# Image convolution block on one core: F(4,3) for two of three convolutions, and the next band's attention begun a step early

## The reference

```python
stk = _neighborhood(x)                        # the 9 shifted views
q = einsum('bhwd,de->bhwe', x, Q_P)
k = einsum('bhwkd,de->bhwke', stk, K_P)
v = einsum('bhwkd,de->bhwke', stk, V_P)
scores = einsum('bhwke,bhwe->bhwk', k, q) * mask
alpha = softmax(scores, axis=-1)
t = x + einsum('bhwk,bhwke->bhwe', alpha, v)
t_in = t
t = relu(conv(t, ff1_kernel) + ff1_bias)      # 64 -> 64
t = relu(conv(t, ff2_kernel) + ff2_bias)      # 64 -> 128
t = relu(conv(t, ff3_kernel) + ff3_bias)      # 128 -> 64
return t_in + t
```

## Time and profile before

| | |
|---|---|
| time, median of 3 runs | 2644.49 us (2639.14 to 2647.08) |
| time of the profiled execution | 2641.18 us |
| its span, first to last instruction | 2639.0 us |
| TensorE matmul busy | 2451.5 us, 93% of the span |
| VectorE busy | 1892.5 us, 72% |
| ScalarE busy | 1183.0 us, 45% |
| mean granted TensorE clock | 0.978 of 2.4 GHz |
| DMA | 311.68 MB, mean 118 GB/s |

### The profile page before, as it was taken

The page is one execution under the profiler, slowest core; times in us unless marked ns, Lnnn a source line. Parts: engine busy times, 40 slices in busy tenths (PEclk is TensorE's granted clock), DMA queues, the critical chain, the costliest instruction groups (busy, mean ns, idle before and its releaser), DMA issues.

```text
span 2639.0 us, 54500 instructions
## 1 busy us (share of the span) xinstructions
PE 2451.5 (93%) x19992; PEld 1300.4 (49%) x19992; DVE 1892.5 (72%) x2767; ACT 1183.0 (45%) x3171; POOL 15.4 (1%) x23
## 2 busy tenths in 40 slices
PE   5999999998899999999889999999988999999997
PEld 3545554554455555545354555455445554554543
DVE  4777777775577777777667777777756777777775
ACT  2544444543454444444344444444435444544433
POOL 2000000000000000000000000000000000000000
PEclk7999999999899999999989999999999999999999
DMA  4433443443344434433244344344423443444343
GB/s 117 134 117 114 121 132 107 124 129 99 98 128 126 132 100 118 140 115 116 87 135 120 109 121 134 112 119 126 133 78 118 122 133 107 123 129 124 107 121 99
DMA packets 217442, 311.68 MB, mean 118 GB/s; under 512 B 15460, under 2 KB 149412, under 8 KB 210724
## 3 DMA queue, kind: packets, MB, share of 16 engines
q1 hardware_dynamic: 217324, 310.12, 40.6%
HBM read 135.47 MB, written 33.82 MB: 64 GB/s over the span
## 4 chain that ended last, share of the span: by engine, by line
PE 71%; DVE 15%; issue 8%; ACT 4%; DVEq 1%; DMA 0%; SPq 0%; ACTq 0%
PE conv_banks L430 26%; PE conv_banks L444 18%; PE conv_banks L407 9%; DVE work L736 6%; PE conv_banks L411 4%; DVE dtl L714 3%; PE mix_bank L384 3%; PE score_banks L369 3%; PE mix_bank L395 3%; ACT dth L606 3%; PE score_banks L358 2%; DVE tf L685 2%; DVE work L698 2%; PE score_banks L350 1%; PE score_banks L366 1%
## 5 line engine op out<-in xcount | busy, mean ns | idle before, releaser
L444 PE MATMUL conv_banks<-du,w2f 64*128 64x512 f32 (+2 forms) x3264 | 745.9, 588 | 57.6 <-DVE work L736 49.0
L430 PE MATMUL conv_banks<-dodd,w3f 128*64 128x512 f32 (+1 forms) x1656 | 499.0, 577 | 10.8 <-DVE dodd L698 10.8
L430 PE MATMUL conv_banks<-deven,w3f 128*64 128x512 f32 (+1 forms) x1656 | 492.0, 567 | 4.2 <-DVE deven L698 3.7
L444 PEld LDWEIGHTS conv_banks<-du,w2f 64*128 64x128 f32 x3264 | 294.7, 190 | 377.6 <-issue 256.4
L533 ACT ACTIVATE prob<-score_banks,negmax 128x100 f32<-128x100 f32 x1040 | 344.9, 360 | 177.8 <-DVE negmax L665 177.8
L726 DVE TENSOR_TENSOR work<-conv_banks,m_sb 128x512 f32<-128x512 f32 (+3 forms) x273 | 179.7, 658 | 327.3 <-PE conv_banks L444 262.6
L736 DVE TENSOR_TENSOR work<-conv_banks,work 128x1024 f32<-128x1024 f32 (+3 forms) x273 | 312.3, 1165 | 60.2 <-PE conv_banks L430 40.6
L563 ACT COPY m_sb<-conv_banks 128x512 f32<-128x512 f32 (+3 forms) x273 | 146.9, 564 | 376.4 <-PE conv_banks L430 165.1
L606 ACT CAST dth<-work 128x1024 fp32r<-128x1024 f32 x130 | 136.1, 1047 | 303.0 <-DVE work L698 302.0
L430 PEld LDWEIGHTS conv_banks<-deven,w3f 128*64 128x64 f32 x1656 | 171.8, 137 | 155.0 <-issue 109.3
L430 PEld LDWEIGHTS conv_banks<-dodd,w3f 128*64 128x64 f32 x1656 | 149.0, 136 | 189.5 <-issue 148.8
(11 more groups left out here) (82 smaller groups left out, 2719.3 us busy)
## 6 DMA issues: line engine op xcount, KB each, us to landing
xk<-x_keys SPq DMA_DIRECT2D x66, 800.0 KB
xc<-x_bands SPq DMA_DIRECT2D x67, 650.0 KB, 5.5
dodd<-dodd SPq DMA_DIRECT2D x68, 512.0 KB, 2.9
xr<-x_bands SPq DMA_DIRECT2D x264, 128.0 KB, 4.8
kept<-tf SPq DMA_DIRECT2D x129, 256.0 KB, 5.0
out<-work SPq DMA_DIRECT2D x60, 512.0 KB, 2.6
dth<-dth SPq DMA_DIRECT2D x68, 256.0 KB, 2.3
dtl<-dtl SPq DMA_DIRECT2D x68, 256.0 KB, 2.4
```

What stands on the lines that cost most here:

```text
L430: return nc.tensor.matmul(bank[rows, lo * 128:hi * 128], w3f[:, m, s, odd * C:odd * C + C], source[:, lo + s // 2:hi + s // 2, m], start=s ...
L444: return nc.tensor.matmul(conv_banks[:, bank_of(which, j), lo * 128:hi * 128], w2f[rows, STREAMS[j], 2 * (which == EVEN) + s], du[rows, lo ...
```

## The change

Convolutions 1 and 2 go from F(2,3) to F(4,3): six streams of a quarter of the width, two to a bank, so three banks instead of four, and four outputs of six products. Both multiply whole fp32; the high and low parts of convolution 1 are gone. VectorE forms the six streams from a first set of differences (`differences`) and then `outer4`, `far4` and `near4`, and the four outputs with `u_middle`, `u_four`, `u_outer` (convolution 1) and `y_middle`, `y_four`, `y_outer` (convolution 2, even and odd rows in one operation). Convolution 3 stays as it was, in its own buffer (`sums3`). r and the first scores of the next band are made in the step before (`nxt`), the r product now in the scores' banks. ScalarE multiplies the probabilities by the inverted sums (`norm`, one copy with a scale for each of four patches), VectorE only inverts (`invert`). The sum with x is one operation. The shared counters `dve_read` and `relu_done` become one semaphore for each use.

The order of each engine, and the new functions, cut to the core:

```diff
             def step(G, k, b, q, par, att):      # SP
-                sp.wait_ge(tile_done, filled(G, CONV1, 3))
-                for t in (dth, dtl):
-                    sp.dma_start(t[:, 0:1].bitcast(F32), t[:, RP:RP + 1].bitcast(F32)).then_inc(t_kept, 16)
+                sp.wait_ge(tile_done, filled(G, CONV1, 2))
+                sp.dma_start(dt[:, :, 0:1], dt[:, :, RP:RP + 1]).then_inc(t_kept, 16)
...
-                store(G, k)
                 if att:
                     sp.wait_ge(mixed, b * 2 + 2)
                     load_xk(b + 1)
-                    sp.wait_ge(t_ready, b * 2 + 2)
+                store(G, k)
+                if att:
+                    sp.wait_ge(t_ready, b + 1)
...
-                sp.wait_ge(tile_done, filled(G, EVEN, 3))
-                sp.dma_start(du[:, 0:1], du[:, RP:RP + 1]).then_inc(u_kept, 16)
+                sp.wait_ge(tile_done, filled(G, EVEN, 2))
+                sp.dma_start(du[:, :, 0:1], du[:, :, RP:RP + 1]).then_inc(u_kept, 16)
```

```diff
+            def conv1_pair(G, k, b, j):          # TensorE
+                if j == 0:
+                    pe.wait_ge(y_mid, before(G))
+                    pe.wait_ge(dt_done, b * 5)
+                    pe.wait_ge(t_kept, G * 16 + 16)
+                elif j == 2:
+                    pe.wait_ge(y_out, before(G))
+                bank = conv_banks[:, BANK1[j]]
+                taps = [(1, 1, 0, RP), (0, 0, 1 if k == 0 else 0, RP)] if k < BANDS else [(0, 0, 0, 1)]
+                for m in range(2):
+                    for n, s, lo, hi in taps:
+                        last = nc.tensor.matmul(bank[:, m * 256 + lo * 64:m * 256 + hi * 64], w1f[:, 2 * j + m, n],
+                                                dt[:, 2 * j + m, lo + s:hi + s],
+                                                start=m == 0 and n == taps[0][0], stop=m == 1 and n == 0)
+                last.then_inc(tile_done, 1)
...
             def begin2(G, k, j):
                 if j == 0:
                     pe.wait_ge(act_read, act_reads(G, CONV3))
+                    pe.wait_ge(o_mid, this(G))
+                    pe.wait_ge(du_done, G * 5 + 10)
+                elif j == 1:
+                    pe.wait_ge(o_out, this(G))
+                else:
                     pe.wait_ge(act_read, act_reads(G, EVEN))
+                for m in range(2):
+                    for s in range(2):
+                        even = tap2(k, EVEN, j, m, LOWER, s, m == 0 and s == 0, False)
+                        odd = tap2(k, ODD, j, m, UPPER, s, m == 0 and s == 0, False)
...
             def end2(G, k, j):
+                pe.wait_ge(half_done, G * 6 + (2 * j + 2))
+                for m in range(2):
+                    odd = tap2(k, ODD, j, m, LOWER, 1, False, m == 1)
+                    even = tap2(k, EVEN, j, m, UPPER, 0, False, m == 1)
```

```diff
+            def norm(b, g):                      # ScalarE
+                act.wait_ge(inv_done, b * GROUPS + (g + 1))
+                for a in range(GROUP):
+                    last = nc.scalar.activation(prob[:, g % 2, a], prob[:, g % 2, a], ACT.Copy,
+                                                scale=expinv[:, g % 2, a:a + 1])
+                last.then_inc(prob_ready, 1)
...
+            def differences(src, slots, done):   # VectorE
+                p = parts_sb[:, :, 0:slots]
+                nc.vector.tensor_tensor(p[:, 1:3], columns(src, slots, 3, 4), columns(src, slots, 1, 2),
+                                        ALU.subtract).then_inc(done, 1)
+                nc.vector.tensor_tensor(p[:, 0:4:3], columns(src, slots, 2, 5), columns(src, slots, 0, 3),
+                                        ALU.subtract).then_inc(done, 1)
+                for n in range(2):
+                    nc.vector.scalar_tensor_tensor(p[:, 4 + n], columns(src, slots, 1 + n), -4.0,
+                                                   columns(src, slots, 3 + n), ALU.mult, ALU.add).then_inc(done, 1)
+            def outer4(to, slots, done):         # one of 2 x 256 elements
+                nc.vector.scalar_tensor_tensor(to[:, 4:6, 1:1 + slots], p[:, 0:2], -4.0, p[:, 2:4],
+                                               ALU.mult, ALU.add).then_inc(done, 1)
+            def far4(to, slots, done):           # two of 256
+                for m, factor in ((3, 2.0), (1, -2.0)):
+                    nc.vector.scalar_tensor_tensor(to[:, m, 1:1 + slots], p[:, 1], factor, p[:, 2],
+                                                   ALU.mult, ALU.add).then_inc(done, 1)
+            def near4(to, slots, done):          # two of 256
+                for m, op in ((2, ALU.add), (0, ALU.subtract)):
+                    nc.vector.tensor_tensor(to[:, m, 1:1 + slots], p[:, 5], p[:, 4], op).then_inc(done, 1)
...
+            def y_middle(G, k):
+                dve.wait_ge(act_read, act_reads(G, EVEN))
+                dve.wait_ge(tile_done, filled(G, EVEN, 1))
+                banks = conv_banks[:, BANK2[1]:BANK2[1] + 2].rearrange("c o (h n) -> c o h n", h=2)
+                nc.vector.tensor_tensor(y_even[:, :, :, at], banks[:, :, :, at], y_copy[:, :, :, at], ALU.add)
+                nc.vector.tensor_tensor(y_odd[:, :, :, at], banks[:, :, :, at], y_copy[:, :, :, at],
+                                        ALU.subtract).then_inc(y_mid, 1)
+            def four(to, even, odd, n, done):    # y_four on 512 elements, u_four on 256
+                if n == 0:
+                    op = nc.vector.tensor_tensor(to(0), even(0), even(1), ALU.add)
+                elif n == 2:
+                    op = nc.vector.scalar_tensor_tensor(to(2), even(1), 4.0, even(0), ALU.mult, ALU.add)
+                else:
+                    op = nc.vector.scalar_tensor_tensor(to(n), odd(1), 2.0 if n == 1 else 8.0, odd(0),
+                                                        ALU.mult, ALU.add)
+                op.then_inc(done, 1)
```

More of the change, by code:

```diff
@@ L403, in conv1_tile @@
                 taps = [(1, 1, 0, RP), (0, 0, 1 if k == 0 else 0, RP)] if k < BANDS else [(0, 0, 0, 1)]
-                pe.wait_ge(dt_high, b * 2 - (1 - part))
-                for w in (w1h, w1l):
+                for m in range(2):
                     for n, s, lo, hi in taps:
-                        nc.tensor.matmul(bank[:, lo * 128:hi * 128], w[:, m, n], dth[:, lo + s:hi + s, m],
-                                         start=w is w1h and n == taps[0][0], stop=False)
-                pe.wait_ge(dt_low, b * 2 - (1 - part))
@@ L565, in relu_conv1, with relu4 @@
+            def relu4(to, rows, src, lo, hi, shift):
+                return nc.scalar.activation(
+                    to[rows, lo:hi, :, 1:1 + W].rearrange("c s i (w n) -> c n s i w", n=4),
+                    src[rows, :, lo * 64:hi * 64].rearrange("c n (s i w) -> c n s i w", i=2, w=WT4),
+                    ACT.Relu, bias=shift)
             def relu_conv1(G, k):
-                act.wait_ge(dve_read, outer_read(G, CONV1))
-                act.wait_ge(d_done[CONV1], parts(G, 1, 1))
+                act.wait_ge(u_summed, G * 4 + 4)
+                act.wait_ge(u_out, this(G))
+                act.wait_ge(du_done, G * 5 + 5)
@@ L729, in outer, with columns @@
-            def outer(G, k, which, behind=0):
-                lo, hi = pairs(which, k)
-                m03 = conv_banks[:, bank_of(which, 2):bank_of(which, 3) + 1:2 if which in (ODD, EVEN) else 1,
-                                 lo * 128:hi * 128]
-                both = sums[which][:, lo:hi].rearrange("c s i (w n) -> c n (s i w)", n=2)
-                dve.wait_ge(tile_done, filled(G, which, 3) if not behind else G * FILLS + (fill_of(which, 3) + 1 - FILLS))
-                dve.wait_ge(dve_read, middle_read(G, which, behind))
-                nc.vector.tensor_tensor(both, m03, both, ALU.add).then_inc(dve_read, 1)
+            def columns(src, slots, *at):
+                if len(at) == 1:
+                    return src[:, 0:slots, :, at[0]:at[0] + W - 3:4]
+                first = at[0] - (at[1] - at[0] == 1)
+                view = src[:, 0:slots, :, first:first + W].rearrange("c s i (w m) -> c m s i w", m=4)
+                return view[:, 1:3] if first < at[0] else view[:, 0:4:3]
@@ L738, in inputs, with o_outer @@
+            def o_outer(G, k):
+                lo, hi = pairs3(k)
+                m03 = conv_banks[:, 2:4, lo * 128:hi * 128]
+                both = sums3[:, lo:hi].rearrange("c s i (w n) -> c n (s i w)", n=2)
+                dve.wait_ge(tile_done, filled(G, CONV3, 3))
+                dve.wait_ge(o_mid, this(G))
+                nc.vector.tensor_tensor(both, m03, both, ALU.add).then_inc(o_out, 1)
             def inputs(G, k, which, part, behind=0):
                 if part == 0:
-                    dve.wait_ge(relu_done, relus(G, which, behind))
```

600 lines of the change are left out of this document (320 added, 280 removed).

## The result

The kernel after takes 2798.01 us (2793.82 to 2801.05) against 2643.05 before: ratio 1.0585, interval 1.0563 to 1.0607. It is 5.9% slower, 155 us, where 2565 us and a gain were forecast; the time is above the range's end of 2690.

The account below looks back on a forecast made before the run. TensorE, busy 93%, bounds the kernel; the new loop sets full steps at 37.9 us. Four pairs give -83, prologue and tail +9: -74 on 2641.2 us makes 2567, stated as 2565, range 2495 to 2690.

Parts of the forecast that it names:

- the cost of the added operations on VectorE and ScalarE: Per step, VectorE net about +1.4 us, to 30 of 38; ScalarE loses high-part casts, gains 16 small scaled copies.
- Rival (d): Longer loop from dearer matmuls, scalar_tensor_tensor, late norm(3) or du: steps 38.5 to 39.8 us, centre 2630; chance 0.22.
- rival (c): TensorE's clock falls behind each step's 2.3 us gap, costing 1 to 4 us a step: 2705 us; chance 0.17.
- The row that warned of it: Old trace: a 1.5 us gap behind 1.3 us of narrow matmuls was followed by a granted clock of 0.50.
- steps 14 and 15: Band steps near an image pair's end, 15 without attention: together 65.7 us instead of 73.9.
- step 16: Band step with one row pair at an image pair's end: about 35.5 us instead of 43.1.
- the loop through scores, maxima, exponentials, copies, y_middle and norm: From next band's scores to turn(0), 6.8 us with TensorE waits of 2.3 and 0.6; full step 37.9 us.
- Convolution 1 in whole fp32: 12 whole fp32 matmuls on 256 columns, 24 instructions at 0.2275 us each: no gain, no loss.
- Convolution 2's pairs: 36 pairs of 256 columns at 0.215 us: 7.75 us a step against 10.3, 2.55 less.
- Rival (b): TensorE stays full if exponentials and copies come early enough: step 35.2 us, 2437 us in all; chance 0.10.
- rival (e): Weight loads not covered by 256-column matmuls: 2.2 us in 64 steps, 2700 us; chance 0.06.
- The sentence of the Trainium skill on loads: Loads overlap running matmuls only when the row group differs; convolution 1 would pay an estimated 2.2 us more a step.

Follow-up runs that it names:

- relu_rows: Kernel after with the relus of convolutions 1 and 2 writing four neighbours, each read from another plane 1 KB apart: 2807.5 us, ratio 1.0619.
- all_dense: Kernel after with relus of convolutions 1 and 2 writing, and VectorE's differences reading, 32 neighbouring elements (columns permuted): 2609.4 us, ratio 0.9876.
- dense_filled: all_dense plus three matmuls of no use in the gap before convolution 2's third pair: 2581.3 us, ratio 0.9766.
- the planes: Kernel after, reordered against the loop, with relu outputs of convolutions 1 and 2 kept as four quarter-width planes: 2490.3 us, ratio 0.9417.
- copies_first: Kernel after with ScalarE's two copies of convolution 2's middle stream moved ahead of the next band's exponentials: 2850.7 us, ratio 1.0781.

## Why the prediction was wrong

The step that failed is the cost of the added operations on VectorE and ScalarE. The prediction counted elements and took the durations of the earlier trace rows for them, the relus as before and the differences as plain sums ("lower bound and choice are the sum's time"). It looked at their number and never at their access patterns. The runs showed 2.16 us for 1.15 (three relus a step, 3.0 us of ScalarE), 1.11 for 0.69 and 0.63 for 0.42 (four and four a step, 2.5 us of VectorE). Taking the sum's time for scalar_tensor_tensor was right where the elements are neighbours (0.417 for 256, 0.683 for 512). Its upper bound, half again as long, about met the strided one, by luck, since the reason for the excess was another; for the relus no bound was set, since they were not taken as changed. Taking the strides away gave 189 of the 233 us by which the time exceeded 2565, and brings it into the stated range (2609); filling the gap alone does not (2754). Rival (d), a longer loop, had the right direction: norm(3) is late, and turn(1) waits 1.45 us for it. It allowed tenths and steps up to 39.8 us; the step became 41.1.

The Trainium skill states the rule (SBUF — State Buffer, Door 1: The DMA port swizzle, the note on SBUF cachelines): lines of 16 bytes, and two touches of a line are needed for full bandwidth. The trace agrees: every fourth fp32 element is one touch a line, and costs 2.16 against 1.15 us. The same note says that one can stride over 4 fp32 elements for free; here exactly that step nearly doubles a relu's time, while a step of 2 (`middle` of the kernel before, 0.689 us for 512) is free, and the measurement decides. relu_rows shows the same cost, 2.12 us, for reads 1 KB apart.

The second error was a chance, not a step: rival (c). Its mechanism, a gap of 2.3 us and then half clock, happened; the sum left it out, at a chance of 0.17. The row that warned of it was nearer than the prediction took it: it read 1.5 us off its window, but the idle time behind the narrow matmuls of the kernel before was 1.77 us, as long as the 1.71 among full-width ones that did no harm:

```profile
1323.03 0.37 PE L366 MATMUL score_banks<-eye_sb 64*128 64x2 f32 x1 [1.77 <-DVE prob L674]
```

The gap filled gives 44 us on the kernel after and 28 on all_dense (2609 to 2581). The price was some 0.7 us a step (44 us over 60 steps) and not 1 to 4, since the matmuls lose some 1.95 us behind a gap (4.74 for 2.79) but half of it only takes the place of the wait for norm(1); in all_dense the fall also comes in only part of the steps. What decides in which steps the clock falls stays open. By the rule of the Trainium skill that the prediction set beside (c) (TensorE: Matmul & The Clock Gate, Why this matters for your kernels) these gaps would be harmless; the falls behind gaps of 2.1 and 2.5 us contradict it.

What is left, 2581 to 2565, is 16 us, or 4 a pair, of errors that partly cancel. In dense_filled a full step is 38.0 us for 37.9 forecast, steps 14 and 15 together 67.1 for 65.7, step 16 38.0 for 35.5, step 0 31.6 for 33 and step 1 35.4 for 35.2; step 16 is the largest miss. So the loop through scores, maxima, exponentials, copies, y_middle and norm was read rightly, and so was that it takes away the gain of TensorE's lighter work: all_dense waits 2.12 us before the third pair (forecast 2.3) and 0.56 before turn(0) (forecast 0.6). In the kernel after the first wait is 2.52, since the strided differences stand before the maximum, which starts 0.6 us behind the scores for 0.2; the second is hidden by the fall of the clock. Reordered against this loop, the same instructions run in 2604, with the planes in 2490. Convolution 1 in whole fp32 costs nothing, 8 matmuls in 1.83 us (1229.12 to 1230.95), 0.229 each for 0.2275. Convolution 2's pairs take 0.232 for 0.215, 0.6 us a step more. `norm` takes 1.2 us for 1.05.

That the full step came out within 0.1 us is partly luck. In dense_filled turn(1) starts 14.62 us after turn(0) (1171.64 to 1186.26), when norm(3) is ready, for the 14.5 forecast; but by then TensorE had been idle for 0.75 us, where the prediction had it arrive at 14.6. Its work ahead of turn(1) was put too high, and the wait and the dearer convolution 2 took the difference up. Rival (b), TensorE staying full, needed another order; rival (e) is refuted by the same pace of convolution 1. The sentence of the Trainium skill on loads that the prediction set beside this pace stands in the page's section The mechanism, not in the one named, and that section also lets a load run ahead when it goes to the background weight buffer; only its narrower sentence is contradicted here.

Each part, taken back alone from the kernel after, gives more or less of the 155 us lost: the strides 189, the clock's fall behind the gap 44, the scaling on ScalarE 71. They overlap, so they don't add up. And with every stride left in, another order alone gives 194: the strides cost so much because they lie on the loop of this order.

## What to carry to other kernels

Before giving a new operation the duration of an old one, write down its innermost step in bytes on each side; a transform that saves matmuls pays for it in the layouts that interleave its outputs. Where two engines hand work to each other across the end of a step, follow that loop for one whole turn with measured durations: here it gave the step to 0.1 us once the strides and the fall of the clock were taken away (with misses inside that cancelled), and told which reordering would help. Moving one member of such a loop (copies_first) moves the wait, and a wait can be worse in its new place than in the old.

## What the hardware showed that was not expected

A 1024-element fp32 relu on ScalarE takes 1.15 us with neighbouring elements, 2.16 when it writes one in each 16 bytes, and 2.12 when it writes neighbours but reads 1 KB apart. VectorE pays 1.11 against 0.69 us for 512 elements and 0.635 against 0.417 for 256, read one in each 16 bytes. TensorE's clock fell to its lower level behind gaps of 2.1 to 2.5 us that come shortly after the narrow score matmuls, in some steps and not in others with the same gap (in all_dense 35 of 64 third pairs ran below 1.00), and work of no use in the gap made the kernel 44 us faster.
